# K^T by a DRAM round trip and VectorE block turns, four projection banks, and the centring of X on VectorE, in a float32 graph layer

## The reference

```python
z_l = h @ W_lang.T ; z_g = h @ W_grav.T ; v = h @ W_V.T
zn  = z_l / max(norm(z_l), EPS)
A_l = max(zn @ zn.T, 0) * not_eye
d2  = max(sq + sq.T - 2 * z_g @ z_g.T, 0)       # sq = row sums of z_g**2
A_g = exp(-d2 / (2 * sigma**2)) * not_eye
K   = w_l * rowstochastic(A_l * adj) + (1 - w_l) * rowstochastic(A_g * adj)
out = (K @ v) @ W_O.T
x   = layernorm(x + out)
```

## Time and profile before

| | |
|---|---|
| median of 3 runs | 718.54 us (718.18 to 722.65) |
| the profiled execution's own time | 718.95 us |
| its span, first to last instruction | 717.2 us |
| PE busy | 695.4 us, 97% |
| DVE busy | 499.9 us, 70% |
| ACT busy | 373.6 us, 52% |
| mean busy share of the 16 DMA engines by the main queue | 42.5% |
| mean granted TensorE clock | 0.993 |

### The profile page before, as it was taken

One profiled execution on the slowest core, in us unless ns is written; L12 is line 12 of the kernel. 1 busy time (PEld: TensorE's weight loads), 2 busy tenths in 40 slices (PEclk: granted clock), 3 DMA queues, 4 the chain that ended last, 5 costly groups with the idle time before them and its releaser, 6 DMA issues.

```text
span 717.2 us, 10995 instructions
## 1 busy us (share of the span) xinstructions
PE 695.4 (97%) x3146; PEld 574.5 (80%) x3146; DVE 499.9 (70%) x1350; ACT 373.6 (52%) x707; POOL 122.8 (17%) x282
## 2 busy tenths in 40 slices
PE   9899999999999999999999999999999999999973
PEld 7688888888888888888888888888888888888852
DVE  4553877768677777778777776867777777866762
ACT  4333445646546554655645554654655464555545
POOL 3301011120212111030211112021211103021112
PEclk9999999999999999999999999999999999999998
DMA  9220534535553544444543445445443454353222
GB/s 288 49 60 32 153 105 117 154 110 156 142 150 113 151 131 124 154 124 125 152 138 120 132 131 151 125 126 154 136 137 122 124 154 124 96 154 96 67 89 95
DMA packets 105013, 90.75 MB, mean 127 GB/s; under 512 B 11040, under 2 KB 79136, under 8 KB 104992
## 3 DMA queue, kind: packets, MB, share of 16 engines
q1 hardware_dynamic: 104432, 88.93, 42.5%
q0 software_dynamic: 288, 1.05, 0.5%
q10 hardware_dynamic: 272, 0.52, 0.2%
HBM read 57.93 MB, written 32.54 MB: 126 GB/s over the span
## 4 chain that ended last, share of the span: by engine, by line
PE 95%; DVE 2%; ACT 1%; issue 1%; DMA 0%; POOL 0%; ACTq 0%; POOLq 0%; DVEq 0%
PE bank L956 90%; PE bank L1071 2%; PE bank L978 2%; PE bank L999 1%; DMA out_y<-y 0%; DVE p_lo L687 0%; ACT y L597 0%; ACT m_hi L510 0%; DVE y L863 0%; DVE m_lo L703 0%; ACT junk_a L589 0%; DVE work L793 0%; DVE hT_raw L673 0%; DVE hT_lo L681 0%; ACT v_hi L543 0%
## 5 line engine op out<-in xcount | busy, mean ns | idle before, releaser
L956 PE MATMUL bank<-hT_lo,m_hi 128*128 128x512 f32 x512 | 168.0, 389 | 0.0
L543 ACT CAST p_hi<-bank 128x512 fp32r<-128x512 f32 x128 | 74.6, 583 | 128.1 <-PE bank L956 128.1
L746 DVE TENSOR_TENSOR p_lo<-bank,p_hi 128x512 fp32r<-128x512 f32 x128 | 87.7, 686 | 57.8 <-ACT p_hi L543 56.3
L956 PE MATMUL bank<-hT_hi,m_lo 128*128 128x512 f32 x320 | 124.5, 389 | 0.0
L956 PEld LDWEIGHTS bank<-hT_lo,m_hi 128*128 128x128 f32 x512 | 96.1, 188 | 19.9
L956 PE MATMUL bank<-p_hi,hT_hi 128*128 128x512 f32 x256 | 101.2, 395 | 0.0
L956 PE MATMUL bank<-wvo_hi,hT_hi 128*128 128x512 f32 x256 | 100.5, 393 | 0.0
L956 PE MATMUL bank<-wvo_hi,hT_lo 128*128 128x512 f32 x256 | 100.4, 392 | 0.0
L956 PE MATMUL bank<-wvo_lo,hT_hi 128*128 128x512 f32 x256 | 100.1, 391 | 0.0
L956 PE MATMUL bank<-p_lo,hT_hi 128*128 128x512 f32 x256 | 100.0, 390 | 0.0
L543 ACT CAST v_hi<-bank 128x512 fp32r<-128x512 f32 x64 | 37.5, 587 | 102.4 <-PE bank L956 102.4
(11 more groups left out here) (105 smaller groups left out, 1226.8 us busy)
## 6 DMA issues: line engine op xcount, KB each, us to landing
x_blk<-in_x SPq DMA_DIRECT2D x128, 128.0 KB, 3.1
x_nat<-in_x SPq DMA_DIRECT2D x32, 512.0 KB, 4.5
out_y<-y SPq DMA_DIRECT2D x32, 512.0 KB, 3.1
x_spill<-xs SPq DMA_DIRECT2D x30, 512.0 KB, 4.0
xq<-x_spill SPq DMA_DIRECT2D x120, 128.0 KB, 3.6
r_row<-r_spill SPq DMA_DIRECT2D x32, 128.0 KB, 4.2
work<-in_L_gnn_W_grav SPq DMA_DIRECT2D x2, 512.0 KB, 6.5
y<-in_L_gnn_W_O SPq DMA_DIRECT2D x2, 512.0 KB, 8.3
```

What stands on the lines that cost most here:

```text
L543: nc.scalar.copy(dst, src).then_inc(proj_hi, 1)
L746: nc.vector.tensor_tensor(dst, src, hi.bitcast(F32), ALU.subtract).then_inc(proj_ready, 1)
L956: last = pe.matmul(dst, lhsT, rhs, start=(n == 0), stop=(n == len(steps) - 1))
```

## The change

K^T no longer goes through PE, except for the last pair. `spill_k` writes K to a DRAM tensor, `return_k` reads it back in four DMAs that exchange the blocks, into the part of `work` in which the cosine matrix stood, and `turn_k` on DVE turns every 32 by 32 block. For that the tiles K, cosine and Gaussian get another order of columns (blocks of 32 in turn from the two row tiles); `gram` becomes one instruction of 512 columns for two of 256. The two banks of K^T are given away: projections and values have four, K V has two (`kv_bank[t]`), so that projection k waits for the low part of k - 4. The shift of X by its diagonal moves from ACT's `centre` into DVE's `diagonal`. `spill_x` is two DMAs, and `store_r` writes single elements, since `r_spill` has another order. All five orders of work are written anew. The diff, its core:

```diff
-        kt_hi = sb("kt_hi", [P, 2, NT, N], F32R)
-        kt_lo = sb("kt_lo", [P, 2, NT, N], F32R)
-        x_spill = nc.dram_tensor("x_spill", [2, NT, P, WIDE], F32)
-        r_spill = nc.dram_tensor("r_spill", [2, P, NT], F32)
+        kt_hi = sb("kt_hi", [P, 2, NT, NT, P], F32R)
+        kt_lo = sb("kt_lo", [P, 2, NT, NT, P], F32R)
+        x_spill = nc.dram_tensor("x_spill", [2, P // BLK, NT, BLK, WIDE], F32)
+        k_spill = nc.dram_tensor("k_spill", [2, NT, P, N], F32)
+        r_spill = nc.dram_tensor("r_spill", [2, NT, P], F32)
...
-        proj_bank = bank[0:3]
-        kv_bank = bank[3]
+        proj_bank = bank[0:4]
         x_bank = bank[4:6]
-        kt_bank = bank[6:8]
+        kv_bank = bank[6:8]
...
 
@@ -294,27 +306,46 @@
 
             def spill_x(p, b):
                 sp.wait_ge(centred, upto(p, 4, 2 * b + 2))
-                sp.dma_start(x_spill[b].rearrange("u p f -> p u f"),
-                             xs[:, b].rearrange("p (u f) -> p u f", u=NT)).then_inc(spilled[b], 16)
+                for u in range(NT):
+                    sp.dma_start(x_spill[b].rearrange("i u c f -> u i c f")[u],
+                                 xs[:, b, u * WIDE:(u + 1) * WIDE]).then_inc(spilled[b], 16)
...
+            def spill_k(q, b):
+                if not live(q):
+                    return
+                sp.wait_ge(k_ready, upto(q, 4, 2 * b + 2))
+                sp.dma_start(k_spill[b].rearrange("h p f -> p h f"),
+                             wk(b, KER).rearrange("p (h f) -> p h f", h=NT)).then_inc(k_spilled[b], 16)
...
+            def return_k(q, b):
+                if not live(q):
+                    return
+                sp.wait_ge(k_spilled[b], 16 * (q + 1))
+                run = NT * BLK
+                for j in range(P // BLK):
+                    cols = k_spill[b].rearrange("h (i c) f -> c (h i) f", c=BLK)[:, :, run * j:run * (j + 1)]
+                    sp.dma_start(wk(b, COS)[j * BLK:(j + 1) * BLK].rearrange("c (k f) -> c k f", f=run),
+                                 cols).then_inc(kq_loaded[b], 16)
+
             def store_r(p, b):
                 sp.wait_ge(pool_steps, upto(p, 6, 3 * b + 1))
-                sp.dma_start(r_spill[b], rnorm[:, b]).then_inc(r_stored[b], 16)
+                sp.dma_start(r_spill[b].rearrange("t p -> p t").unsqueeze(2), rnorm[:, b].unsqueeze(2),
+                             allow_slow_non_contiguous=True).then_inc(r_stored[b], 16)
...
 
                 q = p - 1
                 return_x(q, 1)
+                spread_r(q, 1)
+                load_blocks(p + 1, 1)
+                load_x(q, 0)
+                load_x(q, 1)
+                spill_k(q, 0)
                 load_blocks(p + 2, 0)
+                return_k(q, 0)
+                spill_k(q, 1)
                 store(q - 1, 0)
-                load_blocks(p + 1, 1)
-                spread_r(q, 1)
-                load_x(q, 0)
                 store(q - 1, 1)
-                load_x(q, 1)
+                store_r(p, 0)
                 spill_x(p, 0)
-                store_r(p, 0)
+                return_k(q, 1)
+                spread_r(p, 0)
                 return_x(p, 0)
-                spread_r(p, 0)
                 spill_x(p, 1)
                 store_r(p, 1)
...
-            def centre(p, b):
-                act.wait_ge(diag_ready, upto(p, 2, b + 1))
-                for t in range(NT):
-                    rows = x_plain(b)[:, t, G] if is_last(p) else x_of(b)[:, :, :, G, t].rearrange("p u j a -> p (u j) a")
-                    nc.scalar.activation(rows, rows, ACT.Identity, bias=x_diag[:, b, G, t:t + 1]).then_inc(centred, 1)
...
             def kt_hi_part(q, b):
                 if not live(q):
                     return
-                act.wait_ge(kt_done, upto(q, 2, b + 1))
                 if live(q - 1):
                     act.wait_ge(out_done, upto(q - 1, 4, 2 * b + 2))
-                nc.scalar.copy(kt_hi[:, b], kt_bank[b][:].rearrange("p (t n) -> p t n", t=NT)).then_inc(kt_hi_ready, 1)
+                if is_last(q):
+                    act.wait_ge(kt_done, b + 1)
+                    nc.scalar.copy(kt_hi[:, b].rearrange("p t h n -> p h t n"),
+                                   x_bank[b][:].rearrange("p (h t n) -> p h t n", h=NT, t=NT)).then_inc(kt_hi_ready, 1)
+                else:
+                    act.wait_ge(kt_turned, upto(q, 2, b + 1))
+                    nc.scalar.copy(in_kt(kt_hi, b), wk(b, GAUSS)).then_inc(kt_hi_ready, 1)
...
                 proj_hi_part(p, 0)
                 proj_hi_part(p, 1)
+                squares(q - 1, 0)
                 proj_hi_part(p, 2)
-                normalise(q - 1, 0)
                 proj_hi_part(p, 3)
-                gauss(q, 0)
+                proj_hi_part(p, 4)
+                gauss_scaled(q, 0)
                 squares(q - 1, 1)
-                proj_hi_part(p, 4)
                 proj_hi_part(p, 5)
...
                 proj_hi_part(p, 6)
                 proj_hi_part(p, 7)
                 gauss(q, 1)
+                normalise(q - 1, 0)
+                gauss_scaled(q, 1)
+                save_x(p, 0, 0)
+                save_x(p, 0, 1)
                 normalise(q - 1, 1)
                 kt_hi_part(q, 0)
-                turn_hi(p + 1, 1 - parity, 0)
-                save_x(p, 0, 0)
-                save_x(p, 0, 1)
-                gauss_scaled(q, 1)
-                centre(p, 0)
                 save_x(p, 1, 0)
                 save_x(p, 1, 1)
+                if is_last(p):
+                    return
+                turn_hi(p + 1, 1 - parity, 1)
+                proj_hi_part(p, 8)
+                proj_hi_part(p, 9)
                 kt_hi_part(q, 1)
-                proj_hi_part(p, 8)
-                centre(p, 1)
-                proj_hi_part(p, 9)
-                if is_last(p):
-                    return
-                squares(q, 0)
-                turn_hi(p + 1, 1 - parity, 1)
                 proj_hi_part(p, 10)
                 proj_hi_part(p, 11)
-
+                turn_hi(p + 2, parity, 0)
+                gauss(p, 0)
+
+            turn_hi(1, 1, 0)
...
@@ -762,6 +795,9 @@
                 dve.wait_ge(diag_ready, upto(p, 2, b + 1))
                 nc.vector.tensor_scalar(norm2[:, b], x_diag[:, b, L], 2.0, EPS * EPS, ALU.mult,
                                         ALU.max).then_inc(norm2_ready, 1)
+                for t in range(NT):
+                    rows = x_plain(b)[:, t, G] if is_last(p) else x_of(b)[:, :, :, G, t].rearrange("p u j a -> p (u j) a")
+                    nc.vector.tensor_scalar(rows, rows, x_diag[:, b, G, t:t + 1], None, ALU.add).then_inc(centred, 1)
...
             def turn_x(q, b):
 
...
                 if live(q - 1):
-                    dve.wait_ge(k_ready, upto(q - 1, 4, 2 * b + 2))
+                    dve.wait_ge(kt_ready, upto(q - 1, 2, b + 1))
...
                 dve.wait_ge(xT_ready, upto(q, 2, b + 1))
-                for t in range(NT):
-                    dst = wk_h(b, (COS, GAUSS)[g])[:, :, t].rearrange("p h (j a) -> p h j a", a=BLK)
-                    ins = nc.vector.tensor_tensor(dst, dst, x_of(b)[:, :, :, g, t], ALU.add)
-                ins.then_inc(gram_ready, 1)
-
-            def gram_of_bank(q, b, g):
+                dst = wk_k(b, (COS, GAUSS)[g])
+                own = x_of(b)[:, :, :, g].rearrange("p u j t a -> p (u j) (t a)")
+                nc.vector.tensor_tensor(dst, dst, own, ALU.add).then_inc(gram_ready, 1)
...
+            def turn_k(q, b):
+                if not live(q):
+                    return
+                dve.wait_ge(kq_loaded[b], BLKS * (q + 1))
+                dve.wait_ge(k_ready, upto(q, 4, 2 * b + 2))
+                nc.vector.transpose(wk(b, GAUSS).rearrange("p (t k c) -> p k t c", t=NT, c=BLK),
+                                    wk(b, COS).rearrange("p (k t a) -> p k t a", t=NT, a=BLK)).then_inc(kt_turned, 1)
...
                 dve.wait_ge(kt_hi_ready, upto(q, 2, b + 1))
-                nc.vector.tensor_tensor(kt_lo[:, b], kt_bank[b][:].rearrange("p (t n) -> p t n", t=NT),
-                                        kt_hi[:, b].bitcast(F32), ALU.subtract).then_inc(kt_ready, 1)
...
+                if is_last(q):
+                    nc.vector.tensor_tensor(kt_lo[:, b].rearrange("p t h n -> p h t n"),
+                                            x_bank[b][:].rearrange("p (h t n) -> p h t n", h=NT, t=NT),
+                                            kt_hi[:, b].rearrange("p t h n -> p h t n").bitcast(F32),
+                                            ALU.subtract).then_inc(kt_ready, 1)
+                else:
+                    nc.vector.tensor_tensor(in_kt(kt_lo, b), wk(b, GAUSS), in_kt(kt_hi, b).bitcast(F32),
+                                            ALU.subtract).then_inc(kt_ready, 1)
...
-            def k_turn(q, b):
-                if not live(q):
-                    return
-                pe.wait_ge(k_ready, upto(q, 4, 2 * b + 2))
-                if live(q - 1):
```

(82 more changed lines are left out.)

231 lines of the change are left out of this document (121 added, 110 removed).

## The result

The changed kernel takes **855.5 us** (852.43 to 858.45 in 4 runs) against 718.65 of the kernel before on the same chip: a ratio of 1.189, 95% interval 1.183 to 1.195. It is 19% slower; 705.2 was forecast. The profiled execution took 858.45 with a span of 856.7 us. All times are medians of fast runs; one run of experiment 4 was slow and is left out.

A forecast was written before the change was run, and what follows sets the result against it. PE was taken as the bound, so only removed PE slots save time. From the profiled 718.95: -13.4 for K turns in 14 pairs, -1.0 preparation, +1.0 tail give 705.6, or 705.2 as median; range 702.0 to 712.5.

The forecast's parts named there:

- the paragraph on the transfers: SP's order of DMAs in a pair: K's return lands at 32.0, `store_r` at 31.2, X's return at 36.6, all in time.
- the walk: One pair of the new order followed from its first projection: PE never waits, smallest slack 0.6 us, end at 39.90.
- rival C: `store_r` in 4-byte pieces lands late, holding SP and DVE; PE waits for `v_lo`, DVE idle at L853; 736 us, chance 0.05.
- Rival B: K's return in 256-byte pieces lands 0.5 us late in 14 pairs; PE waits for `kt_lo`; 712 us, chance 0.11.
- the slack of 0.6 for value 10: Projection 2 of the next pair: the low part of value 10 ready at 42.0, needed at 42.62, the least slack.
- D: Rival: the smallest slack of 0.6 isn't there, a shift or `gram` being dearer; 0.3 us a pair, 709 us, chance 0.09.
- The loop: The 14 pairs before the last: 28 K turns leave PE, 0.96 us a pair, -13.4 us.
- The ends: Preparation -1.0 us through the fourth bank; last pair with tail +1.0 us, two fewer turns against a later last store.

The follow-up runs named there:

- experiment 4: experiment 1 with the store and spread of the inverse norms r issued by POOL in place of SP; 845.8 us, ratio 1.176.
- experiment 9: experiment 1, 4-byte store kept, with the return of K of batch 1 issued ahead of the output's stores and that store; 797.3 us, ratio 1.108.
- experiment 1: The changed kernel with each spill of X as four DMAs of 32 partitions instead of two of 4x32x512; 805.3 us, ratio 1.117.
- experiment 5: experiment 1 with r stored in 8-byte pieces again, DVE reading the row with a step of two; 711.5 us, ratio 0.989.
- experiment 11: Experiment 10 with, in pair 0, DVE making the low parts of the last two values ahead of the turn of X; 702.8 us, ratio 0.975.
- Experiment 10: experiment 5 with DVE and ACT in the last pair taking pair 14's work ahead of that for which they wait; 705.75 us, ratio 0.981.

## Why the prediction was wrong

- **The step that failed** is the paragraph on the transfers, which priced reshaped DMAs by the medians of their old shapes. It has "`store_r` lands 5.6 later at 31.2", the median of 8-byte pieces, for a store in 4-byte pieces (9.6 measured); it lets the return of X go out at 31.2, behind a spill issued until 27.0, some 4 us as the one DMA of before took (SP waits up to 13.2 for the new two); and it has "Landing takes 3.6: 32.0" for the return of K behind both. In the pair shown, that return is issued 28.6 to 31.2 us after the first projection (27.0 to 28.8 forecast) and lands at 42.1 where 35.1 was the last moment that the walk allowed. The spill's new shape, 4x32x512 for 128x2x512, stood in the rows of order ahead of the prediction and had no term at all: 50 us (23 with the store cured). The store's new pieces were priced in rival C alone: 121 us (94 with the spill cured).
- **Rival C** had the right object and the wrong reach; its sign shows in experiment 9, once the return of K is out of the way. It priced only `store_r`'s own landing (11.2 us; 9.6 is the median measured) and compared that with slack; the larger part is that the transfers beside and behind it, K's return and X's spill, are held up with it. So it gave 736 at 0.05, where the store alone, with the spill cured, gives 805 [experiment 1]. "Against it: the issue no longer stands behind the 512 KB of X's spill" was no argument: the spill and the return of K now stood behind the store.
- **Rival B** came with the sign that was to show it (PE waits for `kt_lo` once a pair), and yet is not the cause: with the same 256-byte pieces the returns land in 2.6 us in experiment 5, and alone 256 KB take 4.42 us for 3.31 to 4.29. The sign was not specific: it says that the return is late, not why. The loss of 7 us that the rule of the Trainium skill on 512 bytes (DMA: Bandwidth & Descriptors, Specifications) would have brought is shown by no run.
- **A stall's price** was taken as its length. At half clock behind it PE loses about half as much again: 6.3 us idle, 2.9 slow, in a pair of after, whose granted clock is 0.92.
- **What held**, as experiment 5 shows: PE unbroken, pairs of 39.89 (39.90 forecast), DVE 32.0 (32.8), ACT 20.3 (20.5), the turn of K 0.70 (0.6 to 0.69), the shifts 0.35 (0.37), DMA share 0.61 to 0.64 (0.60); the slack of 0.6 for value 10 is there, so D falls. The loop gives 14 x 0.97 = 13.6 of the 13.4 forecast.
- **The ends** were off: forecast -1.0 and +1.0. The preparation gives -0.6, but in the ten kernels of the new order the first projection starts anywhere from 40.1 to 43.0, so nothing is measured. Pair 1 loses 1.8, which experiment 11 gives back: in pair 0, which has no K V to cover it, DVE waits for the return of X while the low parts of two values stand behind that wait; the walk took every pair from 1 on as steady. The tail costs 5.0 for 1.0: the walk saw the squares behind the last split, and not that on DVE the turn of K stands behind a wait for r. Experiment 10 moves both and gives 5.1 back, so the share of each stays open. Sum: -0.6 - 13.6 + 1.8 + 5.0 = -7.4, for 7.3 between the spans (709.9 and 717.2).

How 855 is made up against 711.5, from the two traces: the start -1.3; pair 1 20.2 (61.9 for 41.7); thirteen pairs 118.9 (49.04 for 39.89 each); the last pair with the tail 9.1 (82.5 for 73.4). Together 146.9, for 146.8 between the spans.

## What to carry to other kernels

When a tensor's layout in DRAM is changed, write down for each DMA its outermost dimension and its shortest contiguous run, and price it anew: a median landing belongs to a shape. A transfer of 1 KB can hold up more than one of 512 KB, so ask of a slow one what is under way beside and behind it, not only who waits for it; moving it to another engine's queue moves the wait and shields nothing. A change that moves time the wrong way may be a good one with a bad part: here the new order was worth 1.1% once two DMAs were put back, and 2.5% with its ends in order.
